# Products of ones by ones in five waits of TensorE, in the first stage and in banded attention

## The reference, cut to what matters

```
x = x + L0_attn(L0_cond(x, side, side, ...))     # stage 1: linear attention, ternary weights
x = x + L0_ffn(L0_cond2(x, side, side, ...))     # stage 2: top-1 experts
x = x + L1_attn(L1_cond(x, side, side, ...))     # stage 3: banded attention
x = x + L1_ffn(L1_cond2(x, side, side, ...))     # stages 4 to 8 follow in the same way
...
# cond:  base = sigmoid(x) * (num / max(den, 1e-8)), num and den are sums of scans over exp(side)
# L0_attn: h = rmsnorm(x, qkv_norm_w); q, k, v = h @ ternary(qkv_w).T
# L1_attn: xn = (x - mean(x)) * rsqrt(var(x) + 1e-5) * ln_scale + ln_bias
#          q, k, v of 16 global tokens and of xn; softmax in a band of 32 tokens; @ Wo.T; + residual
```

## Time and profile before

| | us |
|---|---|
| median of three runs | 1716.08 |
| the profiled execution's own time | 1716.67 |
| its span, first to last instruction | 1715.4 |
| PE busy | 1517.7 (88%) |
| DVE busy | 1220.5 (71%) |
| ACT busy | 872.2 (51%) |
| POOL busy | 354.6 (21%) |
| mean granted TensorE clock | 0.942 |

### The profile page before, as it was taken

The page is one execution under the profiler, slowest core; times in us unless marked ns, Lnnn a source line. Parts: engine busy times, 40 slices in busy tenths (PEclk is TensorE's granted clock), DMA queues, the critical chain, the costliest instruction groups (busy, mean ns, idle before and its releaser), DMA issues. The chain is left out here.

```text
span 1715.4 us, 16508 instructions
## 1 busy us (share of the span) xinstructions
PE 1517.7 (88%) x5258; PEld 827.2 (48%) x5258; DVE 1220.5 (71%) x1989; ACT 872.2 (51%) x1586; POOL 354.6 (21%) x226
## 2 busy tenths in 40 slices
PE   4997789789899999977999999766888798899998
PEld 1565355448644444434555555323333333467776
DVE  8586477347456447588898988476988999756665
ACT  5554254356423213267888888345856544334443
POOL 1000432224001001000000000000277878113331
PEclk8998899989999999989999999765899999999999
DMA  2002675252110000022121212002000000111110
GB/s 83 1 1 69 233 245 198 66 98 43 68 82 0 0 16 0 9 79 74 25 76 26 76 26 92 12 20 81 0 1 0 1 0 0 42 41 50 48 51 25
DMA packets 45851, 88.22 MB, mean 51 GB/s; under 512 B 10082, under 2 KB 27444, under 8 KB 43462
## 3 DMA queue, kind: packets, MB, share of 16 engines
q1 hardware_dynamic: 40678, 61.48, 12.4%
q0 software_dynamic: 5088, 25.69, 4.4%
HBM read 70.49 MB, written 7.22 MB: 45 GB/s over the span
## 5 line engine op out<-in xcount | busy, mean ns | idle before, releaser
L2957 POOL TENSOR_TENSOR s_bu<-s_rep,s_du 128x1024 f32<-128x1024 f32 x64 | 150.8, 2358 | 561.6 <-ACT s_rep L2825 522.1
L2769 DVE TENSOR_TENSOR_SCAN s_bu<-bank,s_bu 128x1024 f32<-128x1024 f32 x64 | 146.0, 2282 | 10.4 <-ACT bank L2841 6.1
L159 PE MATMUL bank<-e_xs,e_wsp 128*128 128x512 f32 x528 | 127.7, 391 | 0.7 <-issue 0.7
L3054 PE MATMUL bank<-s_bu,ident 128*128 128x512 f32 x256 | 127.1, 620 | 0.6 <-DVE s_dl L2725 0.2
L159 PEld LDWEIGHTS bank<-e_xs,e_wsp 128*128 128x128 f32 x528 | 99.1, 188 | 22.8 <-issue 1.9
L2841 ACT ACTIVATE bank<-s_dl,s_an 128x510 f32<-128x510 f32 x128 | 82.6, 684 | 51.4 <-DVE s_bu L2769 51.3
L159 PE MATMUL bank<-r_am,r_b 128*128 128x512 f32 x240 | 106.0, 592 | 1.4 <-DVE r_am L1722 1.4
L1780 ACT ACTIVATE r_sl<-bank 128x512 f32<-128x512 f32 x28 | 16.7, 597 | 133.1 <-PE bank L159 133.0
L3168 DVE TENSOR_TENSOR e_s<-e_s,bank 128x512 f32<-128x512 f32 (+1 forms) x50 | 34.4, 688 | 69.7 <-ACT e_s L3300 69.7
L159 PE MATMUL bank<-conditioned,g_wqk 128*128 128x512 f32 x160 | 78.1, 613 | 4.1 <-ACT g_th L2222 3.8
L3300 ACT ACTIVATE e_s<-bank 128x512 f32<-128x512 f32 (+1 forms) x50 | 30.0, 599 | 97.1 <-PE bank L159 97.1
(11 more groups left out here) (518 smaller groups left out, 3545.5 us busy)
## 6 DMA issues: line engine op xcount, KB each, us to landing
g_turn<-g_q SPq DMA_DIRECT2D x64, 128.0 KB, 2.3
e_wgu<-in_e_gu SPq DMA_DIRECT2D x22, 256.0 KB, 2.7
b_vw<-b_values SPq DMA_DIRECT2D x48, 64.0 KB, 3.3
e_wd<-in_e_down SPq DMA_DIRECT2D x22, 128.0 KB, 2.6
r_w<-in_r_w SPq DMA_DIRECT2D x3, 896.0 KB, 8.0
g_wqk<-in_g_qk SPq DMA_DIRECT2D x4, 640.0 KB, 3.9
g_wgv<-in_g_gv SPq DMA_DIRECT2D x4, 640.0 KB, 4.0
g_wo<-in_g_wo SPq DMA_DIRECT2D x4, 512.0 KB, 3.5
```

Source lines behind the costliest of these rows:

```text
L159: last = e.matmul(out, lhs, rhs, start=start and n == 0, stop=stop and n == len(pairs) - 1, skip_group_check=True)
L2769: e.tensor_tensor_scan(b, flat(k.pairs[n % 2][:, :, :]), b, 0.0, ALU.mult, ALU.add).then_inc(k["s_scanned"].up(), 1)
L2957: e.tensor_tensor(m.bu[n % m.NBU][:, :, :], m.rep[:, 2 * np:2 * np + 2, :], m.du[:, et, half(h)].unsqueeze(1).to_broadcast([P, 2, HALF]), ...
L3054: summed = e.matmul(banks[6][:, :], k.ident[:, :], m.bu[(n - 1) % m.NBU][:, i, :], start=np == 0 and i == 0, stop=np == m.NP - 1 and i == ...
```

## The change

A helper `keep_busy(k, e, bank, n)` issues n products of the 128x128 tile of ones with the same tile of ones, repeated four times to 512 columns, into a whole bank that nothing reads before it is written anew. It is called at five places: in stage 1 five products ahead of the wait for `ternary_part` and four ahead of the wait for `ternary_ready`; in stage 3 five ahead of the waits for `conditioned`, two ahead of `norm_tensor`'s waits for `squares` and four ahead of the wait for `b_biased`. Nothing is removed or moved, and no wait is added.

```diff
+def keep_busy(k, e, bank, n):
+
+    ones = k.ones[:, :].unsqueeze(1).to_broadcast([P, 4, P])
+    for _ in range(n):
+        e.matmul(bank[:, :].rearrange("p (a t) -> p a t", a=4), k.ones[:, :], ones, start=True, stop=True, skip_group_check=True)
...
     first_num_tensor(k, e, 0)
     first_num_tensor(k, e, 1)
+    keep_busy(k, e, banks[6], 5)
     e.wait_ge(*k["ternary_part"].at(1))
     mm(e, banks[7][:, 0:1], [(k.ones[:, :], m.partq[:, 0:1])]).then_inc(k["ternary_sum"].up(), 1)
     e.wait_ge(*k["squares"].at(1))
     mm(e, banks[0][:, :], [(k.ones[:, :], m.sq[:, c, half(0)]) for c in range(CT)]).then_inc(k["square_sums"].up(), 1)
+    keep_busy(k, e, banks[6], 4)
     e.wait_ge(*k["ternary_ready"].at(1))
     first_den_tensor(k, e, 2)
...
 def banded_tensor(k, e):
     m, banks = k.banded, k.banks
+    keep_busy(k, e, banks[3], 5)
     for h in range(NH):
         conditioned(k, e, 2, h)
         mm(e, banks[h][:, :], [(k.ones[:, :], k.XC[:, c, half(h)]) for c in range(CT)]).then_inc(k["b_sum"].up(), 1)
+    keep_busy(k, e, banks[3], 2)
     norm_tensor(k, e, 2, m.squares())
...
+    keep_busy(k, e, banks[0], 4)
     e.wait_ge(*k["b_biased"].at(1))
```

## The result

The changed kernel takes 1709.0 us (median of 20 runs, 1704.57 to 1717.15) against 1714.66 for the kernel before (20 runs, 1710.18 to 1717.4). The ratio is 0.9971, with a 95% interval of 0.9958 to 0.9984: 5.0 us faster, between 2.7 and 7.2. The forecast was 1709.2, from a gain of 7.2 us. The prediction drew its bound of faster at 3.4 us: the measured gain lies above it, the lower end of its interval, 2.7, does not. The ratios further down leave out one execution of the kernel before, which took 8483 us. The profiled execution of the changed kernel is one of its slower ones: 1713.34 us, span 1712.1, mean granted clock 0.950 (before: 0.942).

What follows compares the result with a forecast made beforehand. The prediction took TensorE's clock, lost in waits of stages 1 and 3, to put cold work on the path. Gains of 2.9, 2.6 and 1.7 us sum to 7.2, forecast 1709.2 us, range 1705.8 to 1713.4.

Steps and rivals of the forecast that it cites:

- The price of a product: Each product of ones takes 0.85 us of TensorE at the full clock, 1.71 as the upper end.
- Stage 1, -2.9 us: Five and four products keep the clock through the sum of squares and denominator 2; queries' copy at 42.6, 2.9 us earlier.
- Stage 3, five products, -2.6 us: Head of stage 3: sums over channels take 3.6 us, not 6.55; VectorE's difference, ScalarE's square and `b_biased` come 2.6 earlier.
- Stage 3, four products, -1.7 us: Ahead of `b_biased`: with the clock kept, queries and keys take 3.4 us where 5.23 passed before; 1.7 us gained.
- The read-back: Stage 3's read-back of the values has 1.2 us of slack; mixing may come 0.5 us late once, counted as zero.
- The sum: -2.9 - 2.6 - 1.7 = -7.2 us over stages 1 and 3, forecast 1709.2 us.
- Rival 1: Only one part arrives: one stage's products miss, or stage 3's gain ends in the read-back (total 4.1 us); chance 0.15.
- Rival 3: Slower: the products don't count for the clock, and those queued before real work run at half speed; 1727.5 us, chance 0.05.
- Rival 2: Given back later: waits in the rest of the run meet the clock's falls otherwise; 1714 to 1717 us, chance 0.10.

Runs made afterwards that it cites:

- e1: The changed kernel without its three calls in stage 3, so stage 1's five and four products alone; 1711.3 us, ratio 0.9980 to the kernel before.
- e3: The changed kernel with GpSimd's residual adds of stage 3 waiting until VectorE has made both differences; 1708.36 us, ratio 0.9961 to the kernel before.
- e7: e3 plus seven products at the end of stage 1, two before the l0_squares wait, five before normed's last; 1706.06 us, ratio 0.9955 to the kernel before.
- e11: The program of e7 once more, on one chip beside e10; 1706.51 us, ratio 0.9943 to the kernel before.
- e6: The changed kernel without the five and the two products at the head of stage 3, the four before b_biased kept; one run of 1705.55 us.
- e2: The changed kernel without its two calls in stage 1, so stage 3's products alone; 1714.62 us, ratio 0.9989 to the kernel before, unclear.
- e10: The program of e3 once more, on one chip beside e11; 1707.59 us, ratio 0.9951 to the kernel before.
- e8: The changed kernel with products of identity by identity in place of ones by ones, in the same five places; one run of 1712.73 us.
- e9: The changed kernel once more, unaltered, for a second profile; 1711.09 us, ratio 0.9971 to the kernel before.
- e4: The kernel before, no products of ones, with GpSimd's residual adds of stage 3 waiting for VectorE's differences; 1714.8 us, ratio 0.9991, unclear.

## Why the prediction was right, and where it was not

*The price of a product.* Right: ten instructions in 4.46 us, sixteen in 7.03, 0.86 us a product at the full clock, and no product ran at half of it.

*Stage 1, -2.9 us.* Right in every step up to the first scores. Root at 33.86 (33.9 forecast), denominator 2 at 38.16 (38.1), copy of the queries at 42.73 (42.6). First scores at 55.52 and not 58.28: -2.76, and within 0.3 us the same in seven more profiles with these two calls (e1, e3, e7 to e11: 55.28 to 55.56). Only e6 has 56.08; there ScalarE's squares, which TensorE waits for, began at 30.49 and not 29.93, later by as much as the scores are. At the end of the stage part of the gain was missing in the profiled pair: VectorE's conditioning of half 1, at the start of stage 2, moved from 163.04 to 161.63, 1.4 us and not the 2.9 forecast.

*Stage 3, five products, -2.6 us.* This step failed. The sums did end 2.5 us earlier against the start of the stage (7.99 and 10.49). I then wrote that the difference of half 1, "at 348.15, 1.94 us", waited on exactly this. It had waited on it to start, but its end was set by GpSimd's adds. The sign was there: the earlier trace rows has this difference with 1.94 us, its twin of the same form took 1.32, and GpSimd's adds ran across both. I read 1.94 as a price and not as a wait inside an instruction. What the runs show in its place: the end of the head is set by the start of GpSimd's adds, 6.7 us before it, as long as the differences run beside them. Gain at that place: nothing, and 0.5 us lost to the later mask.

*Stage 3, four products, -1.7 us.* Right: from projections to values' products 3.54 us (357.31 to 360.85) and not 5.23.

*The read-back.* The mixing was not held by it: from the values' products to VectorE's conditioning of half 1 behind the stage it is 98.48 us before and after, and 98.47 in e3, where the values come 4.9 us earlier. It is longer only in e2 and e10 (101.51 and 99.87), where the output projections took 10.17 and 8.52 us and not 7.13. This conditioning moved by 4.72 us (464.05 to 459.33) when the start of stage 3 had moved by 3.51, so the stage is 1.21 shorter, as at the values' products.

*The sum.* 2.8 + 1.2 = 4.0 us in the two stages, 4.5 where the mask comes in time; runs say 5.0 (2.7 to 7.2). The forecast's 7.2 was 2.6 to 3.1 too large in one term. That its time, 1709.2, still met the 1709.0 measured is luck: it started from 1716.08, the median of three runs, where 20 runs give 1714.66, and the two medians lie 5.7 us apart, 1.2 to 1.7 us more than the two stages' sum, which the interval allows. The gain of 5.0 is the lower end of the 5 to 8.5 that the prediction called its forecast. Its chances for faster don't add up either: 0.62, 0.06 and half of 0.15 are 0.76, and it says 0.79.

*Rivals.* Rival 1 came closest in number: it has 1.2 us for stage 3 and 4.1 in all, the traces 1.2 and 4.0. Its cause, the read-back, is not the one that was found. Rival 3 fell with the first profile, and e8 shows that products of the identity hold the clock as those of ones do; other data were not tried. Rival 2 is real in single executions. In the profiled pair 1.4 us were given back at the end of stage 1 (5.23 against 6.59) and another 1.3 in the router behind it, so that the products after it start at 166.34 and 166.43 and stage 1's gain is used up; the rest of stage 2 then gained 3.4, of which 2.5 at the wait for the load of the sorted tokens (8.50 and 5.98). PE's timelines, before, then after:

```profile
164.32 2.25 PE L897 MATMUL bank<-m_wr,conditioned 128*128 128x8 f32 x16 [1.00 <-DVE conditioned L270]
166.43 3.30 PE L1194 MATMUL bank<-ident,conditioned 128*128 128x128 f32 x16
```

```profile
162.91 3.58 PE L906 MATMUL bank<-m_wr,conditioned 128*128 128x8 f32 x16 [1.01 <-DVE conditioned L270]
166.34 3.33 PE L1203 MATMUL bank<-ident,conditioned 128*128 128x128 f32 x16
```

In e9, the same program, the router's second sixteen take 1.96 us, and over whole runs the gain stays (e1 0.9980, with an interval clear of 1), so it is noise and not a loss of this size. The Trainium skill, "TensorE: Matmul & The Clock Gate", section "What's actually happening", says that the monitor runs freely and is not restarted by the kernel. The two profiles of one program are in keeping with that, 6.59 and 5.52 for the same eight instructions; they don't show what sets the moment.

For the failed step the Trainium skill has a rule that the prediction did not weigh. "SBUF — State Buffer", section "Who interferes with whom": "A DVE instruction with two SBUF inputs contends with a GpSimd instruction that reads SBUF". The runs agree: the difference takes 1.22 us with the adds out of the way (e3) and 3.22 to 3.37 in the changed kernel. Beside the adds it isn't slow as such, for in the kernel before one of 1.32 ran there too. Its end stands 1.08 us behind the end of an add, so how long it takes depends on when it starts.

## What to carry to other kernels

Products of no use in front of a wait paid here where real work right behind the wait was on the path and they fitted the wait; what ran over was paid in full. Before counting a gain through a chain of engines, look at every instruction in it whose duration differs from its twins: it may hold a wait for another engine, and then a faster start gives nothing. When whole runs scatter more than the change is worth, measure distances between two marks inside one stage, over several profiles.

## What the runs showed that was not expected

Executions of one program differ by up to 12.6 us here (1704.57 to 1717.15 after). Stage 2, which no kernel touches, took from 163.8 us (e6, 162.11 to 325.89) to 175.4 (e4, 164.46 to 339.87) between VectorE's second conditioning and the start of stage 3. The windows of it, of e6 and of e4, show two thirds of the cause: granted clock 0.96 and 0.90, TensorE busy 143.5 and 151.3 us for the same 478 instructions, 7.8 of the 11.6 us.

```profile
163.30:325.90 162.60, 143.49 (x478) 81.58 (x478) 96.23 (x152) 67.60 (x105) 49.95 (x47) 0.96 0.59 203
```

```profile
165.70:339.90 174.20, 151.28 (x478) 85.78 (x478) 96.22 (x151) 67.60 (x105) 49.81 (x47) 0.90 0.55 189
```

The rest of it is one wait: e4 stood 6.5 us before the sorted tokens' load, where e6 stood 2.6 at the same instruction, put down to VectorE. Whether that load was late for a reason of its own stays open.
